# Gathering the experts' rows in the loop from places found by one-hot matmuls, in a fused attention and mixture-of-experts kernel

## What is computed

```python
xn = layernorm(x)
# attention: 16 heads of 8, k and v through a latent of 32
q = xn @ Wq + bq;  latent = xn @ Wl + bl
k = latent @ Wk + bk;  v = latent @ Wv + bv
attn = softmax(q k^T * 8 ** -0.5) v @ Wo + bo
# 16 experts, each token takes its best 2
logits = xn @ Wg.T + bg;  top 2, weights = softmax of the two logits
gate, up = (xn @ Wgu[e] + bgu[e]) even and odd columns
gate = min(gate, 7);  up = clip(up, -7, 7)
ffn = sum over the two of weight * (((up + 1) * gate * sigmoid(1.702 gate)) @ Wd[e] + bd[e])
out = x + attn + ffn
```

## Time and profile before

| | |
|---|---|
| median of 3 runs | 464.88 us (464.76 to 465.46) |
| the profiled execution's own time | 465.35 us |
| its span, first to last instruction | 463.6 us |
| mean granted TensorE clock | 0.947 of 2.4 GHz |
| instructions | 9089 |
| busy in the span: PE, DVE, ACT, POOL | 437.4, 379.9, 309.3, 204.0 us |
| moved by DMA | 37.79 MB |

### The profile page before, as it was taken

One profiled execution on the slowest core, in us unless ns is written; L12 is line 12 of the kernel. 1 busy time (PEld: TensorE's weight loads), 2 busy tenths in 40 slices (PEclk: granted clock), 3 DMA queues, 4 the chain that ended last, 5 costly groups with the idle time before them and its releaser, 6 DMA issues.

```text
span 463.6 us, 9089 instructions
## 1 busy us (share of the span) xinstructions
PE 437.4 (94%) x2681; PEld 205.5 (44%) x2681; DVE 379.9 (82%) x757; ACT 309.3 (67%) x356; POOL 204.0 (44%) x238
## 2 busy tenths in 40 slices
PE   0998999999999999999999999999999999999995
PEld 0455444344444444454444454444444443333453
DVE  7569998989898998888898989898989899985112
ACT  1524004588878787787778777878787877677861
POOL 7042767415172636552454447244636274950000
PEclk9978555999999999999999999999999999999997
DMA  5995681362523233321514150504100413300001
GB/s 146 174 161 179 139 196 52 94 195 68 145 52 105 76 76 60 114 76 46 78 59 123 34 101 24 165 24 82 28 6 6 74 18 85 101 2 1 24 24 45
DMA packets 38275, 37.79 MB, mean 82 GB/s; under 512 B 5664, under 2 KB 33414, under 8 KB 37800
## 3 DMA queue, kind: packets, MB, share of 16 engines
q1 hardware_dynamic: 34320, 32.52, 30.7%
q0 software_dynamic: 2944, 4.75, 3.9%
q10 hardware_dynamic: 984, 0.20, 0.2%
HBM read 23.51 MB, written 13.67 MB: 80 GB/s over the span
## 4 chain that ended last, share of the span: by engine, by line
PE 62%; DVE 22%; ACT 8%; issue 5%; DMA 1%; DVEq 0%; ACTq 0%; SPq 0%
PE banks L1013 18%; DVE half_max L833 18%; PE banks L996 15%; PE banks L1065 12%; ACT probs L698 5%; PE banks L1084 3%; PE banks L1086 2%; PE banks L1021 2%; PE banks L931 1%; ACT th L690 1%; PE banks L955 1%; PE banks L1049 1%; DMA y<-in_x 1%; PE banks L924 1%; ACT pv_sb L671 1%
## 5 line engine op out<-in xcount | busy, mean ns | idle before, releaser
L833 DVE TENSOR_REDUCE half_max<-banks 128x1 f32<-128x512 f32 x512 | 321.6, 683 | 33.3 <-PE banks L996 32.6
L698 ACT ACTIVATE probs<-banks 128x1024 f32<-128x1024 f32 x256 | 254.3, 1024 | 112.7 <-PE banks L1065 109.0
L996 PE MATMUL banks<-k_rows,q_rows 62*128 62x512 f32 x512 | 181.9, 468 | 4.1 <-DVE half_max L833 2.4
L1065 PE MATMUL banks<-q_rows,k_rows 64*128 64x512 f32 x512 | 143.4, 456 | 2.5 <-ACT probs L698 1.9
L1013 PE MATMUL banks<-probs,v_pad 128*32 128x512 f32 x1024 | 137.2, 608 | 0.1
L996 PEld LDWEIGHTS banks<-k_rows,q_rows 62*128 62x128 f32 x512 | 82.6, 196 | 91.5 <-DVE half_max L833 78.5
L1065 PEld LDWEIGHTS banks<-q_rows,k_rows 64*128 64x128 f32 x512 | 57.4, 187 | 69.4 <-ACT probs L698 58.9
L580 POOL DMA_INDIRECT moe_table<-x_rows,result_row x48 | 47.9, 998 | 61.5 <-ACT x_rows L686 44.0
L550 POOL TENSOR_TENSOR gate<-gate,w_blk 128x512 f32<-128x512 f32 x12 | 12.5, 1044 | 77.1 <-ACT gate L682 77.1
L540 POOL DMA_INDIRECT x_table<-xn,place_u x32 | 31.2, 976 | 21.1 <-DVE place_u L814 11.6
L1013 PEld LDWEIGHTS banks<-probs,v_pad 128*32 128x32 f32 x1024 | 20.2, 108 | 42.1 <-issue 29.9
(11 more groups left out here) (119 smaller groups left out, 305.3 us busy)
## 6 DMA issues: line engine op xcount, KB each, us to landing
w_blk<-in_wexp SPq DMA_DIRECT2D x48, 193.0 KB, 3.0
q_rows<-q_parts SPq DMA_DIRECT2D x56, 64.0 KB
k_rows<-k_parts SPq DMA_DIRECT2D x56, 64.0 KB
x_table<-blank SPq DMA_DIRECT2D x1, 3096.0 KB, 21.5
x_rows<-x_table SPq DMA_DIRECT2D x12, 258.0 KB, 3.6
q_parts<-q SPq DMA_DIRECT2D x8, 256.0 KB
k_parts<-k SPq DMA_DIRECT2D x8, 256.0 KB
y<-in_x SPq DMA_DIRECT2D x4, 256.0 KB, 4.4
```

The source lines that it names most:

```text
L698: nc.scalar.activation(probs[:, (2 * s + part) % 4, :, :], banks[:, bank:bank + 2, :], ACT.Exp, scale=SCALE).then_inc(slot_free, 1)
L833: nc.vector.tensor_reduce(half_max[:, unit, row, half:half + 1], banks[:, ring_bank(job), :], AX_X, ALU.max).then_inc(ring_free, 1)
L996: pe.matmul(bank, q_rows[slot][rows, half, pair, P * qb:P * qb + P], k_rows[slot][rows, pair, 512 * keys:512 * keys + 512], start=True, st ...
L1065: mm = pe.matmul(banks[:, bank + u, :], k_rows[(unit // 2) % 2][rows, pair, P * kb:P * kb + P], q_rows[(unit // 2) % 2][rows, half, pair, ...
```

## The change

The tokens are stored once as they are, in a DRAM tensor `tokens`, and each group's rows are gathered from it by four indirect DMAs on POOL (`gather`). Groups 0 to 2 are gathered without a wait in the lead-in and the first pairs, the others at the pairs of `GATHER`, in POOL's stream, behind a wait for the slot's results to be out. `x_table`, its clear, the 32 scatters, the row loads and `rows_of` go. Which token stands in which row is found so: DVE splits `place_u` into the row within a block and the block (`place_at`, two bit operations, ahead of `end_block`). POOL makes of them one-hot matrices in bfloat16: `in_block` (which of 48 blocks), `token_in` (the same times the number of tile and choice, and in its other half, by ACT, times the token's partition), and `at_row` (which of 128 rows), 32 operations. PE adds up 32 matmuls of `at_row` and `token_in`, two ahead of each of the maxima k = 26 to 41. ACT copies the result out, nine small POOL operations make row numbers for the gathers (`token_u`) and for the scatters of results (`result_u`).

```diff
-ROWS_IN = {4: -2, 6: -1, 12: 0, 15: 1}
+GATHER = {3: -2, 6: -1, 10: 0, 14: 1}
...
-        iota_b = sb("iota_b", [P, NEXP + 2 + TILES])
+        iota_b = sb("iota_b", [P, P + 1 + 2 * TILES])
...
-            sp.wait_ge(s_blank, 2)
-            sp.dma_start(x_table.rearrange("(n p) d -> p n d", p=P), blank[:, None, :].to_broadcast([P, BLOCKS, XW])).then_inc(s_cleared, 16)
+            sp.wait_ge(s_xn, TILES)
+            sp.dma_start(tokens.rearrange("(t p) d -> p t d", p=P), xn[:, :, :]).then_inc(s_tokens, 16)
...
-            sp.wait_ge(s_scattered, 16 * 2 * TILES)
-            for m in range(SLOTS):
-                load_rows(m)
...
-            pool.wait_ge(s_place, 1)
-            pool.wait_ge(s_cleared, 16)
-            for n in range(2 * TILES):
...
-                pool.indirect_dma_start(x_table, bass.IndirectOffsetOnAxis(place_u[:, k, t:t + 1], 0), xn[:, t, :], None).then_inc(s_scattered, 16)
+            pool.wait_ge(s_place, 3)
+            for i in range(2):
+                link(nc.gpsimd.tensor_copy(place_n[:, i, :], place_at[:, i, :]))
+            link(nc.gpsimd.tensor_tensor(in_block[:, :, :], place_n[:, 1, :].unsqueeze(2).to_broadcast([P, 2 * TILES, BLOCKS]),
+                                         iota_b[:, None, 0:BLOCKS].to_broadcast([P, 2 * TILES, BLOCKS]), ALU.subtract))
+            nc.gpsimd.tensor_scalar(in_block[:, :, :], in_block[:, :, :], 0.0, 1.0, ALU.is_equal, ALU.mult).then_inc(s_hot, 1)
+            pool.wait_ge(s_hot, 1)
+            nc.gpsimd.tensor_tensor(token_in[:, :, :, 0, :].rearrange("p k t b -> p (k t) b"), in_block[:, :, :],
+                                    iota_b[:, P + 1:P + 1 + 2 * TILES].unsqueeze(2).to_broadcast([P, 2 * TILES, BLOCKS]), ALU.mult).then_inc(s_hot, 1)
+            for k in range(2):
+                for t in range(TILES):
+                    last = nc.gpsimd.tensor_scalar(at_row[:, k, t, :], iota_b[:, 0:P], place_n[:, 0, TILES * k + t:TILES * k + t + 1], 1.0,
+                                                   ALU.is_equal, ALU.mult)
+                last.then_inc(s_hot, 1)
+            pool.wait_ge(s_v, CHUNKS)
+            fill_v(0, 0)
+            fill_v(1, 1)
...
+            pool.wait_ge(s_ids, 1)
...
+            def gather(m):
+
+                i = m % SLOTS
+                if m >= SLOTS:
+                    pool.wait_ge(s_res_out[i], 16 * GB * (m // SLOTS))
+                for q in range(GB):
+                    pool.indirect_dma_start(x_rows[:, i, q, :], None, tokens,
+                                            bass.IndirectOffsetOnAxis(token_u[:, GB * m + q:GB * m + q + 1], 0)).then_inc(s_xrows[i], 16)
+
+            pool.wait_ge(s_tokens, 16)
+            gather(0)
...
             def pair(t, p, last):
+                m = SLOTS * (t + 1) + GATHER.get(p, GROUPS)
+                if p == 1 and t == 0:
+                    gather(1)
+                if m < GROUPS:
+                    gather(m)
...
-                        rows_of(SLOTS * t + i)
...
+            act.wait_ge(s_hot, 1)
+            nc.scalar.activation(token_in[:, :, :, 1, :].rearrange("p k t b -> p (k t) b"), in_block[:, :, :], ACT.Copy,
+                                 scale=iota_b[:, P:P + 1]).then_inc(s_rowed, 1)
             move_max(act, 0, TURN_OF_FIRST)
+            act.wait_ge(s_ids_ps, 1)
+            nc.scalar.activation(fetched[:, :, :].rearrange("p w b -> p (w b)"), banks[:, IDS_BANK, 0:2 * BLOCKS], ACT.Copy).then_inc(s_ids, 1)
...
             nc.vector.tensor_copy(place_u[:, :, :], place_f[:, :, :]).then_inc(s_place, 1)
+            dve.wait_ge(s_place, 1)
+            nc.vector.tensor_scalar(place_at[:, 0, :], place_u[:, :, :].rearrange("p k t -> p (k t)"), P - 1, None, ALU.bitwise_and).then_inc(s_place, 1)
+            nc.vector.tensor_scalar(place_at[:, 1, :], place_u[:, :, :].rearrange("p k t -> p (k t)"), 7, None, ALU.logical_shift_right).then_inc(s_place, 1)
...
+            def find_tokens(n):
+
+                pe.wait_ge(s_hot, 3 + n // TILES)
+                pe.wait_ge(s_rowed, 1)
+                mm = pe.matmul(banks[:, IDS_BANK, 0:2 * BLOCKS], at_row[:, n // TILES, n % TILES, :],
+                               token_in[:, n // TILES, n % TILES, :, :].rearrange("p w b -> p (w b)"),
+                               start=(n == 0), stop=(n == 2 * TILES - 1))
+                if n == 2 * TILES - 1:
+                    mm.then_inc(s_ids_ps, 1)
+
             for k in range(4 * LEAD):
                 ahead, m, job = lead_place(k)
                 if k == 4 * KB:
                     pe.wait_ge(s_q1[0], q1_count(0, 0))
+                if 26 <= k < 42:
+                    find_tokens(2 * (k - 26))
+                    find_tokens(2 * (k - 26) + 1)
...
             pe.wait_ge(s_place, 1)
+            pe.wait_ge(s_ids, 1)
```

More of the change, by code:

```diff
@@ L146, in moe_attention_kernel @@
     k_parts = nc.dram_tensor("k_parts", (PG, 2, PARTS, DH, 2, S), F32, kind="Internal").ap()
-    x_table = nc.dram_tensor("x_table", (BLOCKS * P, XW), F32, kind="Internal").ap()
+    tokens = nc.dram_tensor("tokens", (B * S, D), F32, kind="Internal").ap()
     moe_table = nc.dram_tensor("moe_table", (2 * B * S, D), F32, kind="Internal").ap()
@@ L212, in moe_attention_kernel @@
         place_u = sb("place_u", [P, 2, TILES], U32)
+        place_at = sb("place_at", [P, 2, 2 * TILES], U32)
+        place_n = sb("place_n", [P, 2, 2 * TILES])
+        at_row = attn[:, :, :, :].rearrange("p t g n -> p (t g n)").bitcast(BF16).rearrange("p (k t r) -> p k t r", k=2, t=TILES)
+        in_block = sb("in_block", [P, 2 * TILES, BLOCKS], BF16)
+        fetched = sb("fetched", [P, 2, BLOCKS])
+        result_n = sb("result_n", [P, BLOCKS])
+        token_n = sb("token_n", [P, BLOCKS])
+        empty_n = sb("empty_n", [P, BLOCKS])
+        result_u = sb("result_u", [P, BLOCKS], U32)
+        token_u = sb("token_u", [P, BLOCKS], U32)
         ended = sb("ended", [BLOCKS, NEXP])
@@ L472, in turn @@
                             load_back(h)
-                    for places, bring in ((WEIGHTS_IN, weights_in), (ROWS_IN, rows_in)):
-                        m = SLOTS * (t + 1) + places.get(p, GROUPS)
-                        if SLOTS <= m < GROUPS:
-                            bring(m)
+                    m = SLOTS * (t + 1) + WEIGHTS_IN.get(p, GROUPS)
+                    if SLOTS <= m < GROUPS:
+                        weights_in(m)
             for t in range(TURNS):
@@ new lines, in _ @@
+            pool.wait_ge(s_v, CHUNKS)
+            fill_v(0, 0)
+            fill_v(1, 1)
+            pool.wait_ge(s_weighed, 1)
+            for k, hot in ((0, hot1), (1, hot2)):
+                link(nc.gpsimd.tensor_tensor(hot[:, :, :], hot[:, :, :],
+                                             tw[:, 2 + k, :].unsqueeze(2).to_broadcast([P, TILES, NEXP]), ALU.mult))
+            nc.gpsimd.tensor_tensor(cw[:, :, :], hot1[:, :, :], hot2[:, :, :], ALU.add).then_inc(s_cw, 1)
+            pool.wait_ge(s_cw, 1)
@@ new lines, in _ @@
+            pool.wait_ge(s_ids, 1)
+            link(nc.gpsimd.tensor_scalar(result_n[:], fetched[:, 0, :], float(P), -float(P), ALU.mult, ALU.add))
+            link(nc.gpsimd.tensor_tensor(result_n[:], result_n[:], fetched[:, 1, :], ALU.add))
+            link(nc.gpsimd.tensor_scalar(token_n[:], result_n[:], float(B * S), -float(B * S), ALU.is_ge, ALU.mult))
+            link(nc.gpsimd.tensor_tensor(token_n[:], token_n[:], result_n[:], ALU.add))
+            link(nc.gpsimd.tensor_scalar(token_n[:], token_n[:], 0.0, 1.0, ALU.max, ALU.mult))
@@ L923, in _ @@
                 for t in range(4):
-                    last = pe.transpose(banks[:, c, P * t:P * t + P], xn[:, 4 * c + t, 0:D], id_f[:])
+                    last = pe.transpose(banks[:, c, P * t:P * t + P], xn[:, 4 * c + t, :], id_f[:])
                 last.then_inc(s_xt_ps, 1)
```

74 lines of the change are left out of this document (23 added, 51 removed).

## The result

The changed kernel takes **480.55 us** (median of 3 runs, 478.67 to 480.56) against 464.88, ratio 1.032 with a 95% interval of 1.028 to 1.036. It is 15.7 us slower. I had forecast 469.1 us and a range of 465.6 to 472.6. The sign was right and the size was not.

The account below looks back on a forecast made before the run. It took DVE's maxima to bound the stretch ahead of the loop, with PE busy 96 of 97 us in the turns. 0.3 + 2.3 - 0.4 + 1.9 + 0.1 = 4.2 us on 464.88 gave 469.1, range 465.6 to 472.6.

Parts of the forecast that it names:

- Removed work, nothing: Lead-in: dropping the x_table clear, 32 scatters, SP's wait, row loads and casts gives back nothing; all ran beside DVE.
- DVE's two bit operations, +0.3: Ahead of end_block: two bit operations and a wait for place_u add 0.3 us on DVE.
- DVE behind POOL's subtraction, +2.3: Before the maxima: DVE's tw operation (L825 before the change) waits until POOL's in_block subtraction ends, +2.3 us; bounds nothing and 3.1.
- L842, -0.4: Lead-in: this DVE operation took 0.60 us beside POOL's fill_v; with that work moved it gets 0.4 us shorter.
- PE's finds, +1.9: Maxima k = 26 to 41: two small matmuls each make 0.74 us a job against DVE's 0.60, +1.9; bounds nothing and 3.5.
- POOL late with at_row, priced at nothing: Ahead of the finds: POOL's 32 at_row operations at 0.292 us each end by 60.5, so PE never waits.
- my rival at 0.6 each: At_row at 0.6 us each makes PE stand 5.5 us: 474.6 us; chance 0.12 together with tanh waiting in the turns.
- my threshold of 0.45 each: Ahead of the finds: at_row operations under 0.45 us each were to cost nothing.
- The way of the numbers, nothing: From the last find through ACT's copy and nine POOL operations to the gathers: 3.5 us of cover, no cost.
- the clock, nothing: PE's clock stays at 0.50 through 42 to 72 us and no change in time was counted for it.
- The rival in which the finds wake the clock: Small matmuls in the maxima bring full clock back early, so finds cost nothing: 465.4 us, up to 466.5; chance 0.14.
- The loop, +0.1: Turns: gather DMAs on POOL just fit, tightest at pair 10 before ACT's tanh, +0.1 us; bounds 0 and 1.6.

Follow-up runs that it names:

- comparisons to ACT: The changed kernel with the one-hot matrices at_row made by ACT instead of POOL: 472.56 us, ratio 1.017.
- tw ahead: The kernel of comparisons to ACT with the two place_at bit operations put behind tw in DVE's stream: 469.48 us, ratio 1.012.
- fours for pairs: The kernel of tw ahead with finds four at a time ahead of every third maximum from k = 24: 467.57 us, ratio 1.008.

## Why the prediction failed, step by step

By its own sum of +4.2 us, against +15.7:

- **Removed work, nothing**: right. No gather waits for a landing in the lead-in, and the turns are 97.0 us.
- **DVE's two bit operations, +0.3**: about that (place_at at 42.15, end_block at 42.33 in the changed kernel).
- **DVE behind POOL's subtraction, +2.3**: right to 0.1. L850 2.35 us, the first maximum at 45.77 where I said about 45.5, in an execution that was 0.4 late already at place_u (41.93 for 41.51). The edit that takes it away gave 2.8 us at the first maximum, 2.3 counted from place_u. The Trainium skill, "SBUF — State Buffer", section "Who interferes with whom", says that a DVE instruction with two SBUF inputs contends with a GpSimd instruction that reads SBUF. The trace agrees for the subtraction, which held the DVE operation to its end (45.84 and 45.82).
- **L842, -0.4**: the size right, 0.18 for 0.60, the reason wrong. I had POOL idle by then. At 72.41 it was in the middle of its comparisons, and they didn't hold DVE's operation: 0.17 or 0.18 us in all eight traces in which it ran among them, where waiting for the end of a comparison of 0.7 would have shown. By the same section of the Trainium skill, "SBUF — State Buffer", these POOL operations, which read SBUF, would have contended with it; here the measurement decides against the page.
- **PE's finds, +1.9**: a term mis-sized. I had 0.74 us a job; it is 1.00. The two finds take 0.28 and not 0.11, since neither load hides behind anything, and the next load of k_rows 0.29 and not 0.20, in the open, ahead of 0.43 of streaming. Sixteen times 0.40 is 6.4. From the first maximum to pair 0 the changed kernel took 13.0 us more than the kernel before, 7.9 of them the waits for POOL and 0.4 given back by L842, which leaves 5.6 for the finds (the ring's banks cover the rest of the 6.4). That is outside the bound of 3.5 as well. The bound had the small loads in the open and left out the next load of k_rows, and the forecast had that load and no streaming of the small matmuls. For the load the row said 0.28, at this very clock, and I shortened it to 0.20.
- **POOL late with at_row, priced at nothing**: this is the step that failed. "The nearest row 0.292" was a cast, and I took it for a comparison. The comparisons took 0.72 us each and 5.41 for the long one. PE waited 4.85 and 3.03 us. It was my rival at 0.6 each, 474.6 us, at which I said PE would stand 5.5 us; I had given it 0.12 together with another case. The price had no row. The long comparison made it worse: I had counted it at 2.74, as its upper bound, since it has one input, and it took 5.41, so the first at_row began at 54.2. With that start even my threshold of 0.45 each fails: PE was ready for the first find at 60.4, which leaves 0.39 for each of 16 (an estimate).
- **The way of the numbers, nothing; the clock, nothing**: the first right (the nine small operations end at 87.7, the first gathers run 88.3 to 103.1, rows wanted at 111). The clock stayed at the 1.2 GHz level through the finds and came up 6.8 us behind the first scores of pair 0 where it had been 8.5, which gives back some 0.8 us: DVE idles 0.91 us in pair 0 where it idled 1.69. That is luck of the execution and no gain of the kernel: the same kernel run again had it 9.9 us behind, and turned its first x_rows at 111.5 for 110.6. The rival in which the finds wake the clock is out.
- **The loop, +0.1**: right. The tight place, pair 10, in POOL's timeline:

```profile
154.31 0.99 POOL L593 DMA_INDIRECT moe_table<-x_rows,result_u  x1 [0.30 <-issue]
156.82 1.00 POOL L555 DMA_INDIRECT x_rows<-tokens,token_u  x1 [1.53 <-DMA moe_table<-x_rows,result_u]
...
161.95 1.05 POOL L570 TENSOR_TENSOR gate<-gate,w_blk 128x512 f32<-128x512 f32 x1
163.09 0.61 POOL L576 TENSOR_SCALAR gate<-gate 128x512 f32<-128x512 f32 x1
```

The gather starts 2.5 us after the scatter, as counted (2.4), POOL's gate ends at 163.7 and ACT's tanh of it starts at 164.2. It just fits.

The miss is 11.4 us between the medians and 11.0 between the profiled executions: 7.9 of waits for POOL and 3.7 of finds, less the 0.8 of the clock, and 0.4 at place_u, 11.2 in all. The last two belong to these executions and not to the kernels. The runs on the chip with 464.2 us agree. In their times: comparisons to ACT, 8.0; tw ahead, 3.1; fours for pairs, 1.9 (and with them the wait at k = 24 that came new); 3.4 left, which make up the 16.4 between the changed kernel and the kernel before there. From place_u to pair 0, without the clock behind it, the same steps are 8.1, 1.6, 2.8 and 3.1.

## What to carry to other kernels

A moved or added operation is priced by a row of the same operation, and where there is none the sum must stand at both bounds: a comparison on POOL was 2.5 times a cast of its shape, and when 33 of them stand ahead of a wait of PE's, that one number decides. Where the start of a stretch differs between executions, count from a fixed operation in it: from `place_u` to pair 0 the changed kernel took 45.4 us three times, while its times differed by 9%. Small matmuls put in front of large ones cost the loads on either side, so put them in few groups, and start the first group only when its inputs are there. An edit that removes a true wait is worth nothing while a longer one stands beside it: moving tw brought pair 0 no nearer with POOL late, and 1.6 us nearer after.

## What the runs showed of the hardware

- A comparison on POOL (is_equal against a scalar) took 5.41 us at 128x1536 in bf16, 3.5 ns a column, with mult or max behind it alike. A subtraction of two broadcasts took 2.77 at the same size, and a clip of 128x512 0.61, 1.2 ns a column. At 128x128 it took 0.61 us alone and 0.72 with a product, where a cast took 0.29. At 128x48 in f32 (is_equal, mult) took 0.40, (max, mult) 0.38 and (mult, add) 0.23.
- A DVE operation with two inputs in SBUF took 0.18 us in the middle of a row of POOL's comparisons and 2.35 beside POOL's subtraction.
- On ACT the same 128x128 matrix took 0.30 us by Square (16 in 4.78), and Relu over 128x2048 1.91.
- Where POOL issues many indirect DMAs in a row, the chain shows pauses of 1 to 6 us of other engines on some chips: the kernel before takes 478.8 to 482.5 us there for 464, the changed one 525 for 481, and the granted clock falls with them (0.80 in 25 us around two of them).
